# Attention in a fused kernel: the second pair scores and their exponentials issued at the end of the batch ahead

## What is computed

```python
def reference(x, ctx, mask, g_xattn, g_ffn, Wq, bq, Wk, bk, Wv, bv, Wo, bo, gamma, beta, rscale, gate_w, gate_up, down):
    # cross attention of layernorm(x) over ctx
    q, k, v = heads(layernorm(x) @ Wq.T + bq), heads(ctx @ Wk.T + bk), heads(ctx @ Wv.T + bv)
    scores = clip(where(mask, clip(q @ k.T / sqrt(32), -50, 50), -10000), -50, 50)
    probs = softmax(scores);  probs = probs / (probs.sum(-1) + 1e-8)
    delta = clip(rscale, 0, 0.3) * ((probs @ v) @ Wo.T + bo)
    x = x + tanh(g_xattn) * (layernorm(delta) * gamma + beta)
    # mixture of experts on layernorm(x)
    h = layernorm(x)
    w = top2_normalised(softmax(h @ gate_w.T))
    return x + tanh(g_ffn) * sum_e(w[e] * (silu(h @ gate[e].T) * (h @ up[e].T)) @ down[e].T)
```

## Time and profile before

| | us |
|---|---|
| median of 3 timed runs (lowest, highest) | 952.44 (952.05, 953.12) |
| profiled execution, its own time | 952.24 |
| its span, from first to last instruction | 950.5 |
| TensorE busy in the span | 906.3 (95%) |
| VectorE, ScalarE, GpSimd busy | 432.5, 383.7, 268.0 |
| mean granted TensorE clock | 0.981 of full speed |

### The profile page before, as it was taken

One profiled execution on the slowest core, in us unless ns is written; L12 is line 12 of the kernel. 1 busy time (PEld: TensorE's weight loads), 2 busy tenths in 40 slices (PEclk: granted clock), 3 DMA queues, 4 the chain that ended last, 5 costly groups with the idle time before them and its releaser, 6 DMA issues.

```text
span 950.5 us, 14697 instructions
## 1 busy us (share of the span) xinstructions
PE 906.3 (95%) x4333; PEld 729.4 (77%) x4334; DVE 432.5 (46%) x802; ACT 383.7 (40%) x740; POOL 268.0 (28%) x330
## 2 busy tenths in 40 slices
PE   7978999999799999999999999999999999999994
PEld 7756777778678888888888888888888888888883
DVE  5658868577871221721721635422532172136111
ACT  4485757543342222622622625322622262235221
POOL 6136555564411112212212212211311221212211
PEclk9999999997699999999999999999999999999997
DMA  8210222108272112631631543611551263121121
GB/s 315 89 46 1 78 100 77 56 34 316 97 288 44 23 22 39 217 98 33 203 118 33 195 125 111 221 22 22 170 162 22 37 216 101 33 33 22 33 33 22
DMA packets 27811, 92.90 MB, mean 98 GB/s; under 512 B 5456, under 2 KB 5456, under 8 KB 21136
## 3 DMA queue, kind: packets, MB, share of 16 engines
q1 hardware_dynamic: 18576, 72.03, 20.3%
q0 software_dynamic: 8640, 20.62, 11.8%
q10 hardware_dynamic: 576, 0.02, 0.0%
HBM read 73.98 MB, written 18.68 MB: 97 GB/s over the span
## 4 chain that ended last, share of the span: by engine, by line
PE 79%; issue 6%; POOL 5%; DVE 5%; ACT 2%; DMA 1%; DVEq 0%; SPq 0%; POOLq 0%; ACTq 0%
PE bank L259 70%; PE bank L1612 3%; PE bank L1598 2%; POOL ex_lo L824 2%; POOL o_lo L804 1%; DMA raw<-in_w_attn 1%; PE bank L1305 1%; POOL xr L808 1%; PE bank L1417 1%; DVE xr L435 1%; DVE st6h L439 1%; PE bank L1411 0%; PE bank L1353 0%; DVE tok_tile L691 0%; DMA xg<-h_rows,slot_idx 0%
## 5 line engine op out<-in xcount | busy, mean ns | idle before, releaser
L259 PE MATMUL bank<-g_hi,gt_hi 128*128 128x512 f32 x592 | 237.5, 401 | 0.9 <-DVE gt_lo L717 0.9
L259 PE MATMUL bank<-g_lo,gt_hi 128*128 128x512 f32 x592 | 234.1, 395 | 0.0
L259 PE MATMUL bank<-g_hi,gt_lo 128*128 128x512 f32 x592 | 234.1, 395 | 0.0
L747 DVE TENSOR_TENSOR hid<-silu,bank 128x256 f32<-128x256 f32 x148 | 61.4, 419 | 307.0 <-ACT silu L1270 307.0
L1270 ACT ACTIVATE silu<-bank 128x256 f32<-128x256 f32 x148 | 56.5, 382 | 253.1 <-PE bank L259 232.9
L966 POOL COPY g_idx<-slot_idx 128x1 int32 x37 | 6.9, 185 | 470.1 <-ACT w_nxt L1284 470.1
L259 PEld LDWEIGHTS bank<-g_hi,gt_lo 128*128 128x128 f32 x592 | 111.3, 188 | 26.9
L259 PEld LDWEIGHTS bank<-g_hi,gt_hi 128*128 128x128 f32 x592 | 111.3, 188 | 26.3 <-issue 1.1
L259 PEld LDWEIGHTS bank<-g_lo,gt_hi 128*128 128x128 f32 x592 | 111.4, 188 | 25.0
L259 PE MATMUL bank<-dn_hi,hd_hi 128*128 128x512 f32 x296 | 126.8, 428 | 0.0
L259 PE MATMUL bank<-dn_hi,hd_lo 128*128 128x512 f32 x296 | 116.9, 395 | 0.0
(11 more groups left out here) (236 smaller groups left out, 1289.3 us busy)
## 6 DMA issues: line engine op xcount, KB each, us to landing
raw<-in_w_exp SPq DMA_DIRECT2D x48, 1024.0 KB, 5.3
xs<-in_x SPq DMA_DIRECT2D x4, 1024.0 KB, 6.5
out_rows<-xr SPq DMA_DIRECT2D x16, 256.0 KB, 2.1
h_rows<-dh SPq DMA_DIRECT2D x16, 256.0 KB, 2.1
raw<-in_w_attn SPq DMA_DIRECT2D x3, 1024.0 KB, 13.6
xr<-in_x SPq DMA_DIRECT2D x3, 1024.0 KB, 6.0
raw<-in_w_attn SPq DMA_DIRECT2D x4, 256.0 KB, 7.1
rows<-in_b_rows SPq DMA_DIRECT2D x1, 1024.0 KB, 17.2
```

The lines of the kernel that those rows point to most:

```text
L259: mm = eng.matmul(psum, a(k), b(k), start=(first and k == 0 and j == 0), stop=(last and k == n - 1 and j == 2))
L747: dve.tensor_tensor(hid[:, p, :], silu[:, p, :], bank[p][:, 256:512], ALU.mult).then_inc(hid_done, 1)
```

## The change

Scores 1 of the next batch, with clips, exponentials, high and low parts of pairs 2 and 3, move from the turn of their own batch into the end of the turn ahead, after q product 2. The head of a turn then has pairs 0, 1 and 2 with scores 2, then the o product 0, pair 3 and scores 3. On ScalarE, exponentials 4 and 5 stand at the head, `o_copy` 1 and `normalise_x` next, and exponentials 6 and 7 behind them; on GpSimd `ex_low` 6 and 7 stand ahead of `inverse_delta` 1; on VectorE all four `x_low` stand together. In batch 0 the order within the turn stays and only its end is changed. The set of instructions is the same. The parameter `front` goes, since it was always true. Lines that were only re-indented are left out below.

```diff
 # VectorE
+            def batch(b, back):
                 if back:
                     for m in range(KC):
                         normalise(b - 1, m)
+                    clip(b, 4)
+                    clip(b, 5)
                     ln_statistics(b + 1)
                     update_and_residual(b - 1, 0, None)
+                    clip(b, 6)
+                    clip(b, 7)
                     update_and_residual(b - 1, 1, 0)
                     update_and_residual(b - 1, 2, 1)
...
+                for k in range(KC):
+                    x_low(b + 1, k)
                 if back:
                     update_and_residual(b - 1, 3, 2)
                     update_and_residual(b - 1, None, 3)
+                k_low(b + 1)
+                q_low(b + 1, 0)
                 invert_sums(b)
+                q_low(b + 1, 1)
+                clip(b + 1, 0)
+                clip(b + 1, 1)
                 if not back:
                     split_weight(3)
+                v_low(b + 1)
+                q_low(b + 1, 2)
+                clip(b + 1, 2)
+                clip(b + 1, 3)
+                q_low(b + 1, 3)
 # GpSimd
                 if back:
                     for m in range(KC):
                         o_low(b - 1, m)
+                    ex_low(b, 4)
+                    ex_low(b, 5)
                     add_beta(b - 1, 0)
                     add_beta(b - 1, 1)
                     ln_inverse(b + 1)
                     inverse_delta(b - 1, 0)
                     add_beta(b - 1, 2)
+                    ex_low(b, 6)
+                    ex_low(b, 7)
                     inverse_delta(b - 1, 1)
                     inverse_h(b - 1, 0)
...
+                for s in range(4):
+                    ex_low(b + 1, s)
 # ScalarE
                     for m in range(KC):
                         o_high(b - 1, m)
                     o_copy(b, 0, back)
+                    exps(4)
+                    exps(5)
                     o_copy(b, 1, back)
                     normalise_x(b + 1)
+                    exps(6)
+                    exps(7)
+                    normalise_h(b - 1, 0)
                     x_high(b + 1, range(0, 2))
                     normalise_h(b - 1, 1)
+                    o_copy(b, 2, back)
+                    x_high(b + 1, range(2, KC))
...
+                q_high(b + 1, 2)
                 if back:
                     h_copy(b - 1, 3)
+                exp_and_high(b + 1, 2)
+                if back:
                     keep_logits(b - 1, 2)
+                exp_and_high(b + 1, 3)
+                q_high(b + 1, 3)
 # TensorE
                 if back:
                     spread(b - 1, 0)
                     spread(b - 1, 1)
+                    pv(b, 0, True)
+                    spread(b - 1, 2)
+                    spread(b - 1, 3)
+                    pv(b, 1, True)
+                    scores(b, 2)
+                    pv(b, 2, True)
+                    pe.wait_ge(q_l, b * KC + 3)
+                    o_product(b - 1, 0)
+                    pv(b, 3, True)
+                    scores(b, 3)
+                    pe.wait_ge(q_l, b * KC + 4)
+                    o_product(b - 1, 1)
+                    pv(b, 4, True)
+                    o_product(b - 1, 2)
+                    x_transposes(b + 1, range(0, 2))
+                    pv(b, 5, True)
+                    x_transposes(b + 1, range(2, KC))
+                    o_product(b - 1, 3)
...
+                q_product(b + 1, 2)
+                scores(b + 1, 1)
                 if back:
                     h_transposes(b - 1, 3)
                     router(b - 1, 2)
 # TensorE, batch 3
             pv(LAST, 1, True)
-            scores(LAST, 1)
-            o_product(LAST - 1, 0)
             scores(LAST, 2)
             pv(LAST, 2, True)
+            o_product(LAST - 1, 0)
+            scores(LAST, 3)
             pv(LAST, 3, True)
-            scores(LAST, 3)
+            pv(LAST, 4, True)
+            pv(LAST, 5, True)
             o_product(LAST - 1, 1)
-            for s in range(4, PAIRS):
-                pv(LAST, s, True)
+            pv(LAST, 6, True)
+            pv(LAST, 7, True)
             o_product(LAST - 1, 2)
 # ScalarE, batch 3
             o_copy(LAST, 0, True)
-            exp_and_high(LAST, 2)
-            exp_and_high(LAST, 3)
             exp_and_high(LAST, 4)
-            o_copy(LAST, 1, True)
             exp_and_high(LAST, 5)
             exp_and_high(LAST, 6)
+            o_copy(LAST, 1, True)
             exp_and_high(LAST, 7)
```

More of the change, by code:

```diff
@@ L477, in batch @@
                         normalise(b - 1, m)
-                clip(b, 2)
-                clip(b, 3)
-                if front:
+                    clip(b, 4)
+                    clip(b, 5)
                     ln_statistics(b + 1)
-                if back:
                     update_and_residual(b - 1, 0, None)
-                clip(b, 4)
-                clip(b, 5)
-                if back:
+                    clip(b, 6)
+                    clip(b, 7)
                     update_and_residual(b - 1, 1, 0)
                     update_and_residual(b - 1, 2, 1)
-                if front and back:
-                    x_low(b + 1, 0)
-                    x_low(b + 1, 1)
-                clip(b, 6)
-                clip(b, 7)
-                if front:
-                    if not back:
-                        x_low(b + 1, 0)
-                        x_low(b + 1, 1)
-                    x_low(b + 1, 2)
-                    x_low(b + 1, 3)
+                else:
+                    clip(b, 2)
+                    clip(b, 3)
+                    ln_statistics(b + 1)
+                    for s in range(4, PAIRS):
+                        clip(b, s)
+                for k in range(KC):
+                    x_low(b + 1, k)
                 if back:
@@ L825, in ex_low, with batch @@
                                    ALU.subtract).then_inc(e_l, 1)
-            def batch(b, back, front):
+            def batch(b, back):
                 if back:
@@ L854, in batch @@
                     inverse_h(b - 1, 3)
-                if front:
-                    ex_low(b + 1, 0)
-                    ex_low(b + 1, 1)
+                else:
+                    ex_low(b, 2)
+                    ex_low(b, 3)
+                    ln_inverse(b + 1)
+                    for s in range(4, PAIRS):
+                        ex_low(b, s)
+                for s in range(4):
+                    ex_low(b + 1, s)
             pool.wait_ge(setup, 22)
@@ L884, in _ @@
             ex_low(0, 1)
-            batch(0, False, True)
+            batch(0, False)
             with pool.Fori(1, LAST) as b:
-                batch(b, True, True)
+                batch(b, True)
             def last_x_beta(t):
@@ L1128, in batch @@
                     normalise_h(b - 1, 2)
-                if front:
-                    q_high(b + 1, 0)
+                else:
+                    split_weight(3)
+                q_high(b + 1, 0)
                 if back:
@@ L1137, in batch @@
                     normalise_h(b - 1, 3)
-                if front:
-                    q_high(b + 1, 1)
-                    v_high(b + 1)
-                    exp_and_high(b + 1, 0)
-                    exp_and_high(b + 1, 1)
+                q_high(b + 1, 1)
+                v_high(b + 1)
+                exp_and_high(b + 1, 0)
+                exp_and_high(b + 1, 1)
                 if back:
@@ L1435, in batch @@
+                    scores(b, 2)
+                    pv(b, 2, False)
+                    pv(b, 3, False)
+                    scores(b, 3)
+                    pv(b, 4, False)
+                    x_transposes(b + 1, range(0, 2))
+                    pv(b, 5, False)
+                    x_transposes(b + 1, range(2, KC))
+                pv(b, 6, back)
                 if back:
-                    spread(b - 1, 2)
-                    spread(b - 1, 3)
-                pv(b, 1, back)
+                    pe.wait_ge(dgam, b * TT - 1)
```

143 lines of the change are left out of this document (34 added, 109 removed).

## The result

The changed kernel took 967.84 us (median of 4 runs, 966.92 to 968.24) where the kernel before took 952.78 in the same series (952.05 to 956.23): a ratio of 1.0139, interval 1.0119 to 1.0160. It is 15 us slower. The prediction said 960.3, within 955.0 to 964.0: the sign was right, and half of the loss was missing from it. The profiled execution took 968.1 us with a span of 966.3, against 952.24 and 950.5.

A forecast was written before the change was run, and what follows sets the result against it. TensorE, busy 95% of the span, was taken as the bound. Terms of +4.0, +4.2 and -0.3 us gave +7.9 on 952.24, so 960.1, and 0.2 more for the median: 960.3 us, range 955.0 to 964.0.

The forecast's parts named there:

- Part 1: Scores 1 moved behind q product 2: no net loop change, 1.0 us each way, covering a 0.4 us logits wait.
- Part 2: Batch 0 to batch 1: q_high 3 and q_low 3 held behind pairs 2 and 3, normalise 0 late; +4.0 us once.
- Part 3: Loop turns: inverse_delta 1 queued behind ex_low 6 and 7 delays the second x transposes; +2.1 us a turn, +4.2 in all.
- the sum: Whole kernel: +4.0, +4.2 and -0.3 make +7.9 us, with no fall of the clock included.
- Part 4: Last batch: scores 1 and some waits gone, a new 2.2 us wait for o_un ahead of pair 4; -0.3 us.
- The clock: Rival: one or more of three long TensorE waits drops the clock; one fall 962.3 us, two 964.5; chance 0.17.
- a fall in attention: Sign against the forecast: granted TensorE clock falling in attention, where it was expected at 1.00 throughout.
- evidence against a fall: TensorE wholly idle from 246.95 to 249.95 us, still at 2.4 GHz: 3.0 us idle passed at full clock.
- covered by later idle time: Half-clock loss behind spread 2 of batch 1 would be absorbed by later TensorE idle time.
- The size that I gave for one fall: Behind a long wait, 5 us at half speed lose 2.5 us, 1.7 to 2.5 of it on the path.
- Only one of the costs is real: Rival: q_high 3 or inverse_delta is held less than thought; 956.1 or 956.3 us; chance 0.14.
- The early pairs only remove waits: Rival: TensorE loses 3.4 us of waits, giving 949.0 us, if exponential 6 finishes before add_beta 2; chance 0.10.

The follow-up runs named there:

- the early copy: The changed kernel with ScalarE's copy of o_un 1 ahead of exponential 6 in the last batch; 965.20 us.
- filler: The changed kernel with identity transposes added in TensorE's long waits, 48 at the end of batch 0 and 34 ahead of each turn's second x transposes; 963.30 us.
- the orders mended: The changed kernel with batch 0's split_weight(3) and q_high 3 earlier, exponentials 6 and 7 ahead of normalise_x, last batch's copy 1 ahead of exponential 6; 954.40 us.
- the first filling: The changed kernel with fewer identity transposes in TensorE's long waits, 19 at batch 0's end and 18 ahead of each turn's second x transposes; 966.10 us.

## Why the prediction was half of the loss

**Part 1, the scores moved:** nothing gained or lost, and the wait for logits ahead of the last h transposes is gone, as said.

**Part 2, +4.0 us:** right in mechanism and size. Normalise 0 was 4.46 us late, of which 0.57 came from batch 0's clock, so 3.89. With split_weight and q_high 3 moved up, spread 2 was back at 82.11, and 1.1 us were left at GpSimd's o_low.

**Part 3, +2.1 us a turn:** right in mechanism. The second x transposes were 2.09 us later in turn 2 (predicted 2.14). TensorE's wait was 4.16 to 4.50 where 3.6 was worked out. The turn as a whole loses 1.54 to 1.67 us by order; what follows the transposes gives back some 0.4 more than the sum had. Both ways of letting inverse_delta 1 go in time removed it.

**Part 4, -0.3 us:** mis-sized. The wait of 2.2 us was right (2.23), and by order the batch is even up to pair 7: 22.82 us from the first spread to what follows pair 7, against 21.18 before, and 1.58 of these 1.64 us are the clock (3.03 us between the last batches with and without the early copy, less 1.45 of wait). But a step was missing. I followed the copy and not o product 1, whose move takes GpSimd's three additions into VectorE's r_two steps: 1.32 us. I stopped at the copy of the sums and did not follow the batch on to last_spread. That the additions slow those steps was not tested by an edit of its own; it rests on the overlap in the timelines. In all twelve profiles of kernels with this order of the last batch the steps took 0.63 to 0.65 and 1.37 to 1.38 us with additions beside them, and in the earlier batches of the same profiles, with none beside them, 0.28 to 0.29 and 0.42 us.

By order alone the change costs 3.9 + 1.5 + 1.7 + 0.1 + 1.3 = 8.5 us, where the sum said 7.9; with it the time would have been 960.9 us. What else is missing is the clock, but for 0.2 us.

**The clock, left out of the sum and given a chance of 0.17:** this is the step that failed. The prediction had named a fall in attention as a sign that it was wrong. The clock fell behind all four long waits, in both profiles of the changed kernel:

```
at spread 2 of turn 1        2.07 us   with filler against without
behind the transposes, 1     1.45 us   one kernel with and one without the fall
behind the transposes, 2     1.44 us   with filler against without
behind pair 4, last batch    1.58 us   last batch with and without the fall, less the wait
in batch 0                   0.57 us   landmark
sum                          7.1 us
```

8.5 + 7.1 = 15.6 of the 15.8 us by which the span grew. The figures are read from single executions, and the last-batch one is a remainder. The rows were read wrongly in two ways. First, show TensorE idle for 3.0 us with the clock at 1.00 in that window, and I took it as evidence against a fall. It is not: in the changed kernel too the clock still reads 1.00 from 84 to 85, with TensorE idle since 82.6, and 0.61 in the next microsecond. A full clock in idle time said nothing of the work behind it, and in the earlier trace rows what came behind was at 0.50 from 252 on. The Trainium skill (TensorE: Matmul & The Clock Gate, section "HAM oscillation — how this bites in real kernels") describes a loop in which every pass waits, and every pass starts cold again. In the changed kernel the trace agrees: both turns fell, behind waits of 4.50 and 4.16 us. With waits of 1.64 to 2.46 us in the turns of other kernels here most passes did not. Second, I wrote that the part behind spread 2 is covered by later idle time. It is covered on TensorE's own stream, but scores 2 ran in it, and through clip 4, the exponential and GpSimd's ex_low it delayed the very chain for which TensorE waits later. The wait moved along with it, so nothing was absorbed. The size that I gave for one fall, 1.7 to 2.5 us, was somewhat high (1.4 to 2.1 measured); it was their number and their chance that were wrong: with my own figures four falls would have given 967 to 970.

**The rivals.** "Only one of the costs is real" falls: both are, each undone by its own edit. "The early pairs only remove waits" was right in what it removed, and the kernels with GpSimd's inverses or the exponentials first show that it comes to 0.1 and 0.4 us in turn 2 until the idle time is filled; its condition, exponential 6 done ahead of add_beta 2, did not hold (in turn 1 that exponential starts at 103.95, add_beta 2 at 101.54). With the orders mended and o product 3 moved, the kernel reaches 950.0, near the 949.0 which that rival named, but that is another kernel and no support for the rival.

## What to carry to other kernels

When a step moves, list for each in-order queue what stands behind it and follow every moved step, not only the one that looks critical, to the end of the stage: here exponentials moved ahead of q_high 3 held the normalisation, and a product moved behind two pairs slowed VectorE's steps at the end of the batch. A new long TensorE wait should be priced twice. Here the clock fell at each wait of 2.7 to 4.8 us and at some of 2.1 to 2.5 us, and a fall cost 1.4 to 2.1 us beside the wait; if what runs at half clock feeds the chain of the next wait, later idle time does not absorb it. Work moved out of a place leaves a gap there: look for an independent product to fill it.

## What the runs showed of the hardware that was not expected

- The length of the wait alone did not decide whether the clock fell. In the turns and the last batch it fell at 2.12, 2.23, 2.71 and 2.89 us and did not at 1.64, 1.84, 1.93, 2.07, 2.08, 2.37 and 2.46 us; all waits of 3.8 to 4.8 us had a fall.
- In batch 0 it depended on the execution. Behind waits of 1.17 and 0.96 us, 1.9 us apart, it fell at 51 or 52 us in seven profiles (0.77 and then 0.50 in the windows above) and not in others with the same two waits, the kernel before among them. In two profiles (q_high 3 first, the last batch's copy) it fell at 59 us instead, at a wait of 1.71 us, and in the two with filled waits a second time, some 1.5 us behind the end of one of 2.30 us. What tells these apart was not settled.
- VectorE's two small steps on 48 x 256 elements took 1.37 us instead of 0.42 and 0.64 instead of 0.29 while GpSimd's additions ran beside them (seen, not tested by an edit).
- Transposes of the identity ran back to back at 0.11 us apiece, counted from the first start to the start of what follows (48 in 5.15 us, 19 in 1.99), half of what the first filling was sized by; eight of data took 0.79 us so counted (105.70 to 106.49 in the changed kernel).
